# Two score banks by parity, and the keys' parts summed on GpSimd, in a fused attention and feed-forward kernel

## The reference

```python
x = x + L0_xattn(layernorm(x), ctx, ...)   # one bidirectional attention flow
x = x + L0_ffn(layernorm(x), ...)          # 8 gated experts, 2 of them used for a token
x = x + L1_xattn(layernorm(x), ctx, ...)   # 16 heads of 8 columns
x = x + L1_ffn(layernorm(x), ...)          # one product in fp8 values

def L1_xattn(dec, enc, W_q, W_k, W_v, W_o, b_o):   # the layer of this case
    Q = (dec @ W_q).reshape(4, 256, 16, 8)
    K = (enc @ W_k).reshape(4, 256, 16, 8)
    V = (enc @ W_v).reshape(4, 256, 16, 8)
    scores = einsum('bqhd,bkhd->bhqk', Q, K) / sqrt(8)
    out = einsum('bhqk,bkhd->bqhd', softmax(scores), V).reshape(4, 256, 128)
    return out @ W_o + b_o
```

## Time and profile before

| | |
|---|---|
| time, median of 3 runs | 213.25 us (212.55 to 214.83) |
| time of the profiled execution | 213.41 us |
| its span, first to last instruction | 211.6 us |
| mean granted TensorE clock | 0.969 of full speed |
| busy: PE, DVE, ACT, POOL | 181.0, 154.5, 116.8, 58.5 us |
| 0 to 20 us, first norms and loads | PE busy 15.47 us |
| 55 to 135 us, experts and first groups | PE 74.45, DVE 54.52, ACT 35.10, POOL 11.18 |
| 144 to 200 us, groups and the last batch's end | PE 48.45, DVE 47.21, ACT 42.69, POOL 16.35 |

### The profile page before, as it was taken

How to read it: one execution, slowest core, us unless ns; L and a number is a source line. 1 busy time by engine, 2 the same in 40 slices (tenths; PEclk the granted TensorE clock), 3 DMA queues, 4 the chain that set the end, 5 groups by cost and what they waited for, 6 DMA issues and landing times.

```text
span 211.6 us, 4097 instructions
## 1 busy us (share of the span) xinstructions
PE 181.0 (86%) x1300; PEld 139.4 (66%) x1300; DVE 154.5 (73%) x437; ACT 116.8 (55%) x229; POOL 58.5 (28%) x85
## 2 busy tenths in 40 slices
PE   5699799899999999999999678789999999888231
PEld 4389498678799888889899355546555666445110
DVE  2889758667468565654767996799899999965684
ACT  2257467742322222443354289977989797858242
POOL 3714274691000000300220164333223232304400
PEclk9999999999999999999999999999999999999755
DMA  6999300000000000000000000000000000000002
GB/s 221 378 417 377 137 0 2 0 3 0 0 0 5 0 0 3 0 0 0 3 0 0 2 0 5 0 5 0 2 3 0 0 0 0 0 3 0 0 2 99
DMA packets 4225, 8.81 MB, mean 42 GB/s; under 512 B 880, under 2 KB 1904, under 8 KB 3952
## 3 DMA queue, kind: packets, MB, share of 16 engines
q1 hardware_dynamic: 2480, 7.60, 9.3%
q10 hardware_dynamic: 1728, 1.00, 1.6%
HBM read 5.98 MB, written 0.52 MB: 31 GB/s over the span
## 4 chain that ended last, share of the span: by engine, by line
PE 58%; DVE 19%; issue 9%; ACT 8%; POOL 2%; DMA 2%; DVEq 1%; ACTq 0%; POOLq 0%
PE banks L1176 12%; PE bank L1010 7%; PE bank L1012 7%; PE bank L1011 7%; DVE negm L860 6%; PE bank L1207 5%; PE bank L1241 4%; ACT rest L468 2%; PE banks L1012 2%; PE banks L1011 2%; PE banks L1010 2%; DVE stats L610 2%; PE bank L1250 2%; ACT raw L493 2%; DMA xs<-in_x 2%
## 5 line engine op out<-in xcount | busy, mean ns | idle before, releaser
L860 DVE TENSOR_REDUCE negm<-bank 128x2 f32<-128x512 f32 x64 | 42.0, 687 | 2.4 <-PE bank L1207 1.5
L435 ACT ACTIVATE att<-bank 128x512 f32<-128x512 f32 x32 | 19.2, 599 | 38.4 <-PE bank L1012 25.7
L300 POOL TENSOR_TENSOR keyed<-rest,const 32x256 fp32r<-32x256 f32 x32 | 19.5, 608 | 61.2 <-DVE rest L850 49.9
L493 ACT ACTIVATE raw<-banks 128x1024 f32<-128x1024 f32 x32 | 32.5, 1023 | 3.5 <-PE banks L1226 3.2
L1207 PE MATMUL bank<-keyed 128*128 128x512 f32 x64 | 25.9, 447 | 4.1 <-DVE negm L860 1.8
L815 DVE SCALAR_TENSOR_TENSOR xs<-banks,rw,xs 128x128 f32<-128x128 f32 x64 | 18.0, 344 | 5.9 <-PE banks L1176 5.8
L1176 PEld LDWEIGHTS banks<-raw,attT 128*128 128x128 f32 x176 | 21.3, 192 | 0.8
L1176 PE MATMUL banks<-raw,attT 128*128 128x128 f32 x176 | 21.4, 275 | 0.0
L1010 PE MATMUL bank<-xT,w 128*128 128x512 f32 x48 | 19.9, 416 | 1.4 <-DVE xT L744 1.4
L1207 PEld LDWEIGHTS bank<-keyed 128*128 128x128 f32 x64 | 10.7, 188 | 12.7 <-issue 9.4
L1011 PE MATMUL bank<-xT,w 128*128 128x512 f32 x48 | 18.8, 391 | 0.0
(11 more groups left out here) (201 smaller groups left out, 390.2 us busy)
## 6 DMA issues: line engine op xcount, KB each, us to landing
raw<-in_w SPq DMA_DIRECT2D x1, 2048.0 KB, 10.7
keyed<-negm SPq DMA_DIRECT2D x1, 2048.0 KB, 8.8
raw<-in_w SPq DMA_DIRECT2D x1, 1024.0 KB, 9.8
xs<-in_x SPq DMA_DIRECT2D x2, 256.0 KB, 3.4
ctxT<-in_ctxT SPq DMA_DIRECT2D x1, 512.0 KB, 4.6
ctx<-in_ctx SPq DMA_DIRECT2D x1, 512.0 KB, 6.5
wl<-in_wl SPq DMA_DIRECT2D x1, 256.0 KB, 6.8
wqkraw<-in_wq ACTq DMA_DIRECT2D x1, 256.0 KB, 7.1
```

Of the source, the lines that this page charges most:

```text
L300: pool.tensor_tensor(km[rows, g, j, :], ks[rows, g % 2, :], const[rows, C_ZERO:C_ZERO + 1].broadcast_to([QUAD, SEQ]), ALU.add)\
L435: act.activation(silus[:, k, :], bk[2 * k][:, :], ACT.Silu).then_inc(S["silu_s"], 1)
L493: act.activation(probs[:, slot, 2 * r:2 * r + 2, :, :].rearrange("p h k q -> p (h k q)"), pair[r][:, :], ACT.Exp, scale=ATT_SCALE).then_in ...
L860: dve.tensor_reduce(negm[:, g % 2, r // 2, c0:c0 + QUAD + 1:QUAD], bk[1 + r % 2][:, :].rearrange("p (h k) -> p h k", h=2), AX.X, ALU.max, ...
```

## The change

The turn of a group is written once for each engine (`pe_group`, `act_group`, `dve_group`) and all 16 turns are written out, without the loop.

- **Keys.** `stack_keys` on DVE and the two copies on ACT are gone. ACT's `hiK` now carries the factor `C_AK` itself, and ACT copies the full keys into `kraw`. POOL adds `kraw` and `hiK` straight into the four masked copies.
- **ACT's order.** Both exponentials of a group now stand ahead of `proj_hi(m + 3)`.
- **Banks.** Scores 0, 1 and 3 of an odd group go to bank 2 and score 2 to bank 1, and the other way round for an even group; `turn_maxima` uses the bank that the group's scores 0, 1 and 3 had. Score 1 no longer waits for the shifted queries of the group ahead; score 2 does.
- **Turns.** `outputs(m - 2)` is issued in two halves, heads 0 and 1 (`LOW`), then heads 2 and 3 (`HIGH`), with score 1 of group m + 1 between them. The transposes, the normalisation, `output_layer` and `add_attention` of a batch are spread over four groups of the next. The head outputs are kept in a ring of five. The waits for bank 7 are gathered in `bank7_free`.

```diff
-        ks = rest[:, 0:2 * SEQ].rearrange("p (u k) -> p u k", u=2)
+        kraw = rest[:, 0:2 * SEQ].rearrange("p (u k) -> p u k", u=2)
         hiQ = rest[:, 2 * SEQ:3 * SEQ]
-        hiK = rest[:, 3 * SEQ:4 * SEQ]
-        os_ = rest[:, 4 * SEQ:(4 + G) * SEQ].rearrange("p (g q) -> p g q", g=G)
+        hiK = w14[:, :, :].rearrange("p b d -> p (b d)").rearrange("p (u k) -> p u k", u=2)
+        heads_out = rest[:, 3 * SEQ:(4 + G) * SEQ].rearrange("p (n q) -> p n q", n=G + 1)
...
+        def score_bank(m, r):
+            if m == 0:
+                return 2 - r % 2
+            return 2 - m % 2 if r == 2 else 1 + m % 2
+
+        def turn_bank(b, t):
+            return 0 if t == 0 and b >= BATCH - 2 else 7
...
-            def masked_keys(m, g, first):
-                pool.wait_ge(S["ks_s"], m + 1)
-                if not first:
-                    pool.wait_ge(S["s2_ps"], 2 * (m - 3))
-                for j in range(2, HPG):
+            def masked_keys(m):
+                pool.wait_ge(S["k_hi"], m + 1)
+                pool.wait_ge(S["k_raw"], m + 1)
+                if m >= G:
+                    pool.wait_ge(S["s2_ps"], 2 * (m - G + 1))
+                for j in range(HPG):
                     rows = slice(QUAD * j, QUAD * (j + 1))
-                    pool.tensor_tensor(km[rows, g, j, :], ks[rows, g % 2, :],
-                                       const[rows, C_ZERO:C_ZERO + 1].broadcast_to([QUAD, SEQ]), ALU.add)\
-                        .then_inc(S["km_pool"], 1)
-                    pool.wait_ge(S["km_pool"], 2 * m + j - 1)
+                    pool.tensor_tensor(km[rows, m % G, j, :], kraw[rows, m % 2, :], hiK[rows, m % 2, :], ALU.add)\
+                        .then_inc(S["km_s"], 1)
+                    pool.wait_ge(S["km_s"], HPG * m + j + 1)
...
             def proj_hi(m, bank=0):
                 act.wait_ge(S["proj_ps"], m + 1)
-                queries_hi(m, bank)
-                keys_hi(m, bank)
-
-
-            def masked_keys(m, g, first):
-                act.wait_ge(S["ks_s"], m + 1)
-                if not first:
-                    act.wait_ge(S["s2_ps"], 2 * (m - 3))
-                for j in range(2):
-                    rows = slice(QUAD * j, QUAD * (j + 1))
-                    ins = act.copy(km[rows, g, j, :], ks[rows, g % 2, :])
-                ins.then_inc(S["km_act"], 1)
-
-
-            def exps(m, g, r, first, slot=None):
+                act.wait_ge(S["qs_s"], m)
+                act.copy(hiQ.bitcast(r32), bk[bank][:, 0:SEQ]).then_inc(S["q_hi"], 1)
+                if m >= 2:
+                    act.wait_ge(S["km_s"], HPG * (m - 1))
+                act.activation(hiK[:, m % 2, :].bitcast(r32), bk[bank][:, SEQ:2 * SEQ], ACT.Identity,
+                               scale=const[:, C_AK:C_AK + 1], bias=const[:, C_ONE:C_ONE + 1]).then_inc(S["k_hi"], 1)
+                act.copy(kraw[:, m % 2, :], bk[bank][:, SEQ:2 * SEQ]).then_inc(S["k_raw"], 1)
...
-            def o_copy(m, g, bank=7):
+            def o_copy(m, bank=7):
                 act.wait_ge(S["pv_ps"], m + 1)
-                act.copy(os_[:, g, :], bk[bank][:, SEQ:2 * SEQ]).then_inc(S["o_ev"], 1)
-            def act_batch(b, first, last):
...
+                if m >= G and m % G == 1:
+                    act.wait_ge(S["oT_ps"], TPB * (m // G))
+                act.copy(heads_out[:, m % (G + 1), :], bk[bank][:, SEQ:2 * SEQ]).then_inc(S["o_ev"], 1)
+
+            def turned_out(b):
+                act.wait_ge(S["aoT_ps"], b + 1)
+                act.copy(aoT[:, :], bk[7][:, 0:SEQ]).then_inc(S["aoT_ev"], 1)
+
+            def act_group(m):
+                b, g = m // G, m % G
+                if 2 <= m < GROUPS - 1:
+                    o_copy(m - 2)
+                exps(m, 0)
+                if m in (2, 3):
+                    later_norm_hi(g)
+                if m in TURNED_AT:
+                    turned_out(b - 1)
+                exps(m, 1)
+                if m + 3 < GROUPS:
+                    proj_hi(m + 3)
+                if m in (1, 2):
+                    for t in range(TPB * (g + 1), TPB * (g + 2)):
+                        third_scaled(t)
...
-            def dve_batch(b, first, last):
...
+            def dve_group(m):
+                b, g = m // G, m % G
+                more = m + 1 < GROUPS
+                if more:
+                    maxima(m + 1, 0)
+                shifted(m)
+                if more:
+                    maxima(m + 1, 1)
+                if m + 2 < GROUPS:
+                    stack_queries(m + 2)
+                if more:
+                    maxima(m + 1, 2)
+                if m == 0:
+                    sum_moments(1)
+                if m in (2, 3):
+                    later_norm_lo(g)
+                if g == 0 and b >= 2:
+                    add_attention(b - 2, slice(TPB * (b - 2), TPB * (b - 1)))
+                if b > 0 and g == 1:
+                    normalise(b - 1, 0)
+                if 0 < b < BATCH - 1 and g == 2:
+                    normalise(b - 1, 1)
+                if more:
+                    maxima(m + 1, 3)
+                if b == BATCH - 1 and g == 1:
+                    normalise(b - 1, 1)
+                if m == GROUPS - 1:
+                    moments(4, CHUNKS[0], lambda t: dve.wait_ge(S["x3_s"], t // TPB + 1))
+                    add_attention(b - 1, slice(TPB * (b - 1), TPB * b))
...
-            def scores(m, g, r, first):
+            def project(m, bank=0):
+                pe.wait_ge(S["qs_s"], m)
+                b, g = m // G, m % G
+                cols = slice(b * SEQ, (b + 1) * SEQ)
+                for a, src in enumerate((xT, ctxTs)):
+                    ins = three(bk[bank][:, a * SEQ:(a + 1) * SEQ],
+                                (wqk[:, 0, a, g * P:(g + 1) * P], wqk[:, 1, a, g * P:(g + 1) * P]),
+                                (src[:, 0, cols], src[:, 1, cols]), True, True)
+                ins.then_inc(S["proj_ps"], 1)
+
+
+            def scores(m, r):
+                t, half = r // 2, r % 2
                 pe.wait_ge(S["qs_s"], m + 1)
-                if r % 2 == 0:
-                    pe.wait_ge(S["km_act"], m + 1)
-                else:
-                    pe.wait_ge(S["km_pool"], 2 * (m + 1))
-                if r == 1 and not first:
+                pe.wait_ge(S["km_s"], HPG * m + 2 * (half + 1))
+                if r == 0 and m > 0:
+                    pe.wait_ge(S["s1_max"], 4 * m - 1)
+                elif r == 2 and m > 0:
                     pe.wait_ge(S["qa_s"], m)
-                elif r > 1 or not first:
-                    pe.wait_ge(S["s1_max"], 4 * m + r - 1)
-                t, pair = r // 2, r % 2
-                pe.matmul(bk[1 + r % 2][:, :], qs[:, g, t * P:(t + 1) * P],
-                          km[:, g, 2 * pair:2 * pair + 2, :].rearrange("p h k -> p (h k)"),
+                elif r == 3 or (r == 1 and m > 0):
+                    pe.wait_ge(S["s1_max"], 4 * m + (r + 1) // 2)
+                elif r == 2:
+                    pe.wait_ge(S["s1_max"], 1)
+                pe.matmul(bk[score_bank(m, r)][:, :], qs[:, m % G, t * P:(t + 1) * P],
+                          km[:, m % G, 2 * half:2 * half + 2, :].rearrange("p h k -> p (h k)"),
                           start=True, stop=True).then_inc(S["s1_ps"], 1)
...
-            def outputs(m, g, b, first, bank=7, heads=range(HPG), slot=None):
-                pe.wait_ge(S["p_s"], 2 * m + (heads[-1] // 2 + 1))
-                pe.wait_ge(S["v_s"], b + 1)
-                if not first and bank == 7:
+            def outputs(m, heads, bank=7):
+                pe.wait_ge(S["p_s"], 2 * m + heads[-1] // 2 + 1)
+                pe.wait_ge(S["v_s"], m // G + 1)
+                if m > 0 and bank == 7:
                     pe.wait_ge(S["o_ev"], m)
-                if slot is None:
-                    slot = g % 2
+                slot = m % 2 if m < GROUPS - 1 else 2
                 for j in heads:
                     for t in range(TPB):
-                        ins = pe.matmul(bk[bank][QUAD * j:QUAD * (j + 1), SEQ:2 * SEQ], vones[:, t, g * HPG + j, :],
-                                        probs[:, slot, j, t, :], start=t == 0, stop=t == TPB - 1,
-                                        tile_position=(0, QUAD * j))
+                        ins = pe.matmul(bk[bank][QUAD * j:QUAD * (j + 1), SEQ:2 * SEQ],
+                                        vones[:, t, (m % G) * HPG + j, :], probs[:, slot, j, t, :],
+                                        start=t == 0, stop=t == TPB - 1, tile_position=(0, QUAD * j))
...
+            def bank7_free(m):
+                b, g = m // G, m % G
+                if m in (3, 4):
+                    pe.wait_ge(S["x3T_lo"], m - 1)
+                if b >= 1 and g == 2:
+                    pe.wait_ge(S["ao_s"], TPB * (b - 1) + (1 if b < BATCH - 1 else TPB))
+                if 1 <= b < BATCH - 1 and g == 3:
+                    pe.wait_ge(S["ao_s"], TPB * b)
+                if m in (2 * G, 3 * G, GROUPS - 1):
```

(51 more changed lines are left out.)

261 lines of the change are left out of this document (60 added, 201 removed).

## The result

The changed kernel takes 226.09 us (median of 4 runs, 225.58 to 226.57), against 213.76 us (4 runs, 212.55 to 214.83): a ratio of 1.058, 95% interval 1.051 to 1.065. The forecast was 222.6, with a range of 216.5 to 226.5. The profiled execution took 225.58 us, with a span of 223.8, so that 1.8 us lie outside the span as before.

A forecast was written before the change was run, and what follows sets the result against it. PE and DVE were nearly full, so the order inside a turn decides. Turns 2 to 14 sum to 70.57 us against 61.13 (+9.4), turns 0 and 1 give -0.2; span 220.8 plus 1.8 outside makes 222.6 us, range 216.5 to 226.5.

The forecast's parts named there:

- The two halves: PE's outputs in turns 2 to 14: each half takes 0.99 us against 1.02 for all, adding 0.96 a turn.
- first rival: A half of the outputs costs half, 0.51 us, so the kernel gets faster, 209.9 us; chance 8 in 100.
- The rule against the row: PE's outputs: skill's strict program order would make a half cost half; rows show four heads' matmuls at once, so measurement decides.
- The size of a score between narrow matmuls: PE's score between output halves: a step of 0.34 us, though its full duration is 0.47.
- 26 changes: New changes between narrow and wide matmuls on PE: up to 0.13 us more each, 3.4 us, left to the range.
- Turns 0 and 1: Turns without outputs: DVE saves two steps of 0.40 us, gives most back by waiting; -0.2 taken, between 0 and -0.8.
- DVE's waits: Normalisation, attention addition and rounding ahead of the last reduction wait for PE: turns of 5.68, 5.53 and 6.03 us.
- second rival: POOL becomes the bound: copies of 1.28 us, four taking 5.2 us a turn, 223.7 us; chance 2 in 100.
- the price and the cover: POOL's four masked copies: 0.64 us each, some 2.6 together, with 1.2 us of cover before the scores ask.
- The unrolling: Loop's register work dropped on each engine: counted as nothing, 0.1 us for each of 8 looped turns left to the range.

The follow-up runs named there:

- e1: Changed kernel with the 16 output matmuls of a turn in one piece again, ahead of score 1: 213.78 us, ratio 1.000.
- e3: Kernel before with only the outputs split by heads around score 1 of the next group: 226.00 us, ratio 1.056.
- e2: Changed kernel with each half of the outputs holding all four heads for one tile of keys, instead of two heads: 214.66 us, ratio 1.004.
- e6: Changed kernel with 11 spare products of the identity into bank 7 in each of turns 0 and 1: 227.40 us, ratio 1.063.
- e7: On top of e1, score 1 moved ahead of the outputs in one piece: 219.72 us, ratio 1.030.
- e9: On top of e8, DVE's normalisation and addition of the attention moved behind the last reduction: 210.04 us, ratio 0.980.
- e10: On top of e9, the rounding of batches 2 and 3 also moved behind the last reduction: 208.27 us, ratio 0.974.
- e8: On top of e5, ACT's order undone, with the next projection between the two exponentials again: 212.28 us, ratio 0.993.
- e4: Kernel before with only the loop over batches 1 and 2 written out: 212.78 us, ratio 0.993.
- e5: On top of e1, DVE's stacked queries moved back ahead of the reduction of score 1: 212.43 us, ratio 0.994.

## Why the prediction was right

**The two halves** were the deciding step, and it held: 0.99 to 1.00 us for each, from the two rows of 8 matmuls in turn 15 of the kernel before. e1 removes the cost, e3 makes it alone, and e2 shows what most of it consists of: not the number of matmuls in a half, nor the cut, but how many of the four column groups are in use. The first rival (209.9 us) fell with its assumption.

**The rule against the row** went the way of the row. By the Trainium skill, "TensorE: Matmul & The Clock Gate", Part 3, The mechanism, matmuls start strictly in program order; by that rule a half would have cost half. e1, in which the two products of a head follow one another in the program, has 16 in 1.02 us, and e2, in which the heads alternate, has 8 in 0.57: both times fit four column groups side by side, each with its own matmuls one behind another. The records don't name the head, so that the four matmuls begun together belong to four heads is inferred from these times. With that, the rule does not hold for the starts that these traces record.

**The size of a score between narrow matmuls** was the term that was too small. I took its step as 0.34 and put up to 0.13 more for each of 26 changes into the range; it measured 0.43 and 0.42, so 0.09 and 0.08 more, 2.2 us in 13 turns. This explains most of the 0.12 to 0.26 us that were missing in each turn but turn 2. In turns 7 and 11 the projection behind two transposes took 0.80 instead of 0.71, another 0.2 in the two.

**The clock** was not in the prediction at all; it adds 1.0 us in turn 2 of the profiled execution. e6 shows the size. Whether it fell in the executions that were only timed is not known. The three terms, 2.2 + 0.2 + 1.0, make the 3.4 us by which the window is longer than forecast. The range held in part by luck: of the 3.4 us that it set aside for the changes between narrow and wide matmuls only 2.2 were needed, and the clock, for which it had nothing, took what was left. The profiled execution also started its turn of group 0 earlier by 0.9 us, for no reason in the sum.

**Turns 0 and 1** were forecast 0.2 us shorter and came out 0.24 us longer, 8.54 us. That is the clock again, which fell within turn 1: in e2 and e7, in which these two turns have the same order as here and the full clock, they take 8.16 us, 0.14 less than before. In both places together the low clock cost about 1.4 us.

**DVE's waits** in the turns with more in them were right as a mechanism (0.62 us ahead of the reciprocal in turn 6), and e9 and e10 confirm them from the other side: with that work behind the last reduction the same turns lose 0.3 to 0.9 us (e8 against e9 and e10).

**ACT** is not waited for by PE, and its order is worth nothing (e8); POOL waits for its copy of the keys (18.1 us in all) without holding up PE, and DVE for its copy in turns 2 and 3 (2.1 us), as forecast. **POOL** is not waited for in the changed kernel either. From turn 2 to turn 15 PE waited for DVE alone, by its waits:

```profile
PE bank L1182 <- DVE negm L831: 3.8, 9, 0.8
```

So the second rival fell. But the price and the cover were wrong. A copy takes 0.723 us, four 3.1 us, where I had 0.64 and 2.6 by halving a row of 512 columns. Halving lost a part that does not shrink with the columns. The kernel before had a third size that shows it:

```profile
L277 POOL TENSOR_TENSOR wqk<-wqkraw,wqk 128x1024 fp32r<-128x1024 f32 x1 | 2.4, 2406 | 0.0
```

From 1024 to 512 columns it falls by 1.122 us, so half of that again, 0.561, from 1.284 for 512 gives 0.723 for 256, an estimate that meets the measured one. And I had left out the values (L299), which in turns 5, 9 and 13 stand ahead of the copies and wait for the second half of the outputs:

```profile
141.06 3.12 POOL L311 TENSOR_TENSOR keyed<-rest,w 32x256 fp32r<-32x256 f32 x4 [3.04 <-ACT rest L472]
...
147.97 0.40 POOL L299 COPY vones<-vall 128x256 f32<-128x256 f32 x1 [2.42 <-issue]
148.45 3.12 POOL L311 TENSOR_TENSOR keyed<-rest,w 32x256 fp32r<-32x256 f32 x4
```

In turn 4 two copies are there at 142.6 and score 0 starts at 144.73; in turn 5 they are there at 149.97 and it starts at 150.10. The cover there is 0.13 us, not 1.2 (0.14 and 0.10 in turns 9 and 13), so that POOL cost nothing is close to luck, and e7 shows what happens when the scores ask earlier.

**The unrolling**, which I had counted at nothing, is worth 0.7% in the kernel before (e4). In the changed kernel it was not tested apart.

**What the change was worth without the split** is e1: nothing (1.000), and after its other losses are removed 0.6% to 0.7% (e5, e8), which is what e4 gets by the unrolling alone. The keys on POOL took 5.7 us off DVE (L850 in the window), whose busy time there fell by 4.5 us, and ACT's fell by 7.2 us, but the turn's loop ran over PE's outputs, a score and three reductions, and none of these had become shorter. Only in e9 and e10, where the rest of the loop was cleared, do the times fall to 210.0 and 208.3. How much of that needs the keys on POOL was not tried: e9 and e10 have not been made in the kernel before.

## What to carry to other kernels

Here, matmuls that fill a part of the array's columns were paid by the busiest column group, not by their number (four to a group: 1.02 us for 16, 0.99 for 8; two to a group: 0.57 for 8). Cut such a row so that each piece still has all column groups, and look for a row of the same size in the trace before cutting. Cut at all only where it buys more than the cut costs, 0.3 us in this kernel, where a full-width matmul between narrow ones ran for nearly its whole duration before the next began. Price a shorter instruction from two sizes of its kind, not by halving one. And in a loop bound by a chain over two engines, first move away what stands ahead of the chain's last step (here the normalisation ahead of the last reduction) before taking work off engines that only run beside it.

## What the runs showed of the hardware that was not expected

- POOL's addition of two tensors of 32 partitions by 256 took 0.714 to 0.746 us in all 64 instances; with one operand a broadcast column it took 0.608 on average, and the same form with 128 partitions took 0.613 (L254 of the kernel before). The group of the changed kernel:

```profile
L311 POOL TENSOR_TENSOR keyed<-rest,w 32x256 fp32r<-32x256 f32 x64 | 46.3, 723 | 46.6 <-ACT rest L472 42.5
```

- ACT's rounding with a scale and a bias taken from a tensor took 0.590 us for 128 x 256, the one with the bias alone 0.475 before, a plain copy 0.392:

```profile
L470 ACT ACTIVATE w<-bank,const 128x256 fp32r<-128x256 f32 x16 | 9.4, 590 | 0.0
L472 ACT COPY rest<-bank 128x256 f32<-128x256 f32 x16 | 6.3, 392 | 0.0
```

- The granted clock fell to its lower level for some 3 us at turn 2 in the profiled executions of the changed kernel, e1, e4 and e9 (0.50 from 126 to 128 us in all four), in that of e3 a few us earlier (0.72 from 118 to 124 us), and not in those of the kernel before, e2, e5, e6, e7, e8 and e10. What PE did just before does not tell them apart: in the five stretches of 2 us from 116 to 126 us it was busy for 1.27, 1.52, 1.89, 1.03 and 1.91 us in e9, whose clock fell (0.80 in the last of them), and for 1.29, 1.50, 1.90, 1.02 and 1.92 us in e10, whose clock stayed at full. What decides it is open.
